# Key and query biases as one factor, query normalisation on GpSimd, and the statistics of x2 from two accumulators, in the attention loop of a macaron block

## The chip, the cores and the metric

The kernel runs on one core of a Trainium2 chip. The metric is the device time of one execution in microseconds (us), given as the median of several runs. Of the core's engines the text speaks by short names: PE is TensorE, DVE is VectorE, ACT is ScalarE, POOL is GpSimd, and SP is the engine whose queue issues most transfers.

## What is computed

The program is one block of three parts, each with a residual connection and a layer normalisation ahead of it: a mixture of experts, a causal linear attention, and the experts again with the same weights. All values are f32. There are 8 sequences of 1024 rows of 512 numbers, 64 tiles of 128 rows in all. Only the attention and the normalisation behind it are touched here. Cut to what matters:

```
x1 = x + 0.5 * ffn(layernorm(x))
q  = exp(layernorm(x1) @ Wq.T + bq)          # 16 heads of 32
k  = exp(layernorm(x1) @ Wk.T + bk)
v  = layernorm(x1) @ Wv.T + bv
num = q @ cumsum(outer(k, v))                # along the sequence
den = sum(q * cumsum(k))                     # for each head
x2  = x1 + (num / den) @ Wo.T + bo
out = x2 + 0.5 * ffn(layernorm(x2))
```

In num and den every product has one factor of q and one of k in the same dimension, so exp(bq) and exp(bk) can be multiplied in anywhere once. The kernel adds both biases into one tile, BK, at the start, and applies it to one of the two.

## The kernel before

The program has three stages in time: the first gate and experts, with the projections of x for q, k and v computed ahead and put in DRAM (to about 1010 us); the attention loop (to about 1915 us); the second experts, which stream their weights from DRAM again. Each engine runs its own instruction list, written out by hand, and semaphores order them. The change lies in the attention loop.

The loop index n runs over tiles of 128 rows. In one turn of the loop the engines work on several tiles at once: on the products of tile n, on the preparation of tile n + 1 (m in the code), on x2 of tile n - 1 and on the transposes of the normalised x2 of tile n - 2. The names used below are these.

- X1 is the tile after the first experts. PB[.][:, 0], [:, 1] and [:, 2] are q, k and v of a tile. DVE forms X1 and the three sums (L1132, and three adds through the helper L264), which read PSUM banks 4 to 7, and then the statistics of X1 (L1117, L1119, L1121).
- RS is one over the standard deviation, a power on POOL (L1203). ACT takes the exponentials of q and k (L1063, L1066) with it. KH is k rounded to the matmul's format (L1071, ACT), and KL the rest (L1206, POOL).
- UPTO and AFTER are triangular matrices. PE multiplies them with KH and KL into bank 2, which gives the running sum of k. DVE multiplies it with q into PR, reduces it to DEN (L1173), inverts that to RDEN (L1175), and multiplies q by it in place (L264, in the code the line with Q3).
- PE transposes k and q, ACT copies them to KT and QT (L1056, L1059), PE forms the scores S in banks 4 to 7, DVE masks them with TRI into ST (four instructions), and PE forms the attention output (semaphore s_av). ACT copies it to AT and rounds it to ATH (L1084, L1087), POOL forms the rest ATL (L1218), and PE multiplies by WO (12 matmuls `ps<-wo,s`, semaphore s_op).
- X2 is that product plus X1 with BO added (POOL, L1209), a sum on DVE. Its statistics are DVE's L1117, L1119 and L1121, one over its standard deviation POOL's L1214, the shift NM DVE's L1182, and the normalised XN3 ACT's L1093. PE transposes XN3 in the next turn.

PE may start the scores of tile n only when DVE has read banks 4 to 7 for tile n + 1, that is after X1 and the three sums. From n = 10 on every eighth turn also selects the best tokens of a finished sequence on DVE (the maximum, the replacement and the mask, then a turn later the weights), and the turns behind it gather them on PE.

Of the kernel before, what the change touches and what calls it, by code (L numbers as in the profile page):

```python
# [20 lines left out]
def macaron_block(nc, x, Wq, bq, Wk, bk, Wv, bv, Wo, bo, gate_w, gate_b, w1, w2, out):  # L21
    F = mybir.dt.float32
# [8 lines left out]
    EPS = 1e-5  # L31
# [9 lines left out]
    with ctx:  # L41
# [7 lines left out]
        def sem(name):  # L49
            return ctx.enter_context(nc.semaphore(name))  # L50
# [125 lines left out]
        def sems(name, n):  # L176
# [28 lines left out]
            "s_c", "s_x1", "s_tk", "s_tq", "s_tv", "s_x1st", "s_x1ag", "s_x1ve", "s_x1rs", "s_x1b"))  # L205
        s_kb, s_qe, s_ke, s_v, s_ktT, s_kt, s_qtT, s_qt, s_S, s_st, s_av, s_at = (sem(n) for n in (
            "s_kb", "s_qe", "s_ke", "s_v", "s_ktT", "s_kt", "s_qtT", "s_qt", "s_S", "s_st", "s_av", "s_at"))
# [4 lines left out]
        s_op, s_x2, s_x2st, s_x2ag, s_x2ve, s_x2rs, s_x2n, s_g3T, s_xt3, s_lg3, s_L3, s_fin, s_fout = (  # L212
            sem(n) for n in ("s_op", "s_x2", "s_x2st", "s_x2ag", "s_x2ve", "s_x2rs", "s_x2n", "s_g3T", "s_xt3", "s_lg3",
                             "s_L3", "s_fin", "s_fout"))
# [827 lines left out]
        def attention_act(act):  # L1042
# [3 lines left out]
            for v in range(6):  # L1046
                outer_act(act, v)
            for n in range(-2, NT + 9):
                live = 0 <= n < NT
# [3 lines left out]
                if live:  # L1053
                    act.wait_ge(s_ktT, n + 1)
                    act.wait_ge(s_S, 4 * n)
                    nc.scalar.copy(KT, ps[:, 0, :]).then_inc(s_kt, 1)  # L1056
                    act.wait_ge(s_qtT, n + 1)
                    act.wait_ge(s_av, n)
                    nc.scalar.copy(QT, ps[:, 1, :]).then_inc(s_qt, 1)  # L1059
                if nxt:  # L1060
                    act.wait_ge(s_tq, m + 1)
                    act.wait_ge(s_x1rs, m + 1)
                    nc.scalar.activation(PB[m % 4][:, 0, :], PB[m % 4][:, 0, :], ACT.Exp,  # L1063
                                         scale=RS[m % 2]).then_inc(s_qe, 1)
# [44 lines left out]
        def attention_dve(dve):  # L1109
            center_dve(dve)  # L1110
            dve.wait_ge(s_woh, 1)
            tt(WOL, WO, WOH.bitcast(F), ALU.subtract).then_inc(s_wol, 1)
            dve.wait_ge(s_bk, 1)

            def stats(i, src, s_src, s_st_, s_ag, s_ve, n):
                dve.wait_ge(s_src, n + 1)
                nc.vector.bn_stats(ST6[i], src).then_inc(s_st_, 1)  # L1117
                dve.wait_ge(s_st_, n + 1)
                nc.vector.bn_aggr(MV[i], ST6[i]).then_inc(s_ag, 1)  # L1119
                dve.wait_ge(s_ag, n + 1)  # L1120
                nc.vector.tensor_scalar(VE[i], MV[i][:, 1:2], EPS, None, ALU.add).then_inc(s_ve, 1)  # L1121

            for n in range(-2, NT + 9):
# [5 lines left out]
                if nxt:  # L1129
# [27 lines left out]
                if 0 <= n - 1 < NT:  # L1157
# [20 lines left out]
                if 0 <= n - 1 < NT:  # L1178
                    m = n - 1
                    dve.wait_ge(s_x2rs, m + 1)  # L1180
                    dve.wait_ge(s_x2n, m - 1)
# [11 lines left out]
        def attention_pool(pool):  # L1193
            pool.wait_ge(s_bo2, 1)
            for n in range(-2, NT + 2):
                m = n + 1
                if 0 <= m < NT:
                    pool.wait_ge(s_x1ve, m + 1)
                    pool.wait_ge(s_x2rs, n - 2)
                    pool.wait_ge(s_atl, n)  # L1200
                    for s_ in (s_kb, s_qe, s_v):
# [4 lines left out]
                    nc.gpsimd.tensor_tensor(KL, PB[m % 4][:, 1, :], KH.bitcast(F), ALU.subtract).then_inc(s_kl, 1)  # L1206
# [110 lines left out]
```

## Time and profile before

| what | value |
|---|---|
| median of 3 runs | 2622.75 us (2622.47 to 2626.64) |
| span of the profiled execution | 2617.3 us |
| busy: PE, DVE, ACT, POOL | 2133.4, 1008.2, 717.8, 368.0 us |
| instructions on POOL | 389 |
| chain that ended last: PE, DMA, DVE | 47%, 30%, 13% |
| between 1500 and 1600 us, in the loop: PE, DVE, ACT, POOL busy | 82.17, 86.12, 50.97, 36.85 us |

The profile gives the span from the first to the last instruction; it has no device time of its own, and the median of the runs is 5.4 us above the span. The busy shares over the whole span say little of the loop, where the stages behind and ahead of it hardly use DVE or POOL. The last line of the table is the loop alone.

### The profile page before, as it was taken

The numbers are of one execution on the slowest core, as the hardware profiler recorded it, in microseconds if no ns is written. First come the engines' busy times: TensorE is split into PE (matmuls) and PEld (weight loads), VectorE is DVE, ScalarE is ACT, GpSimd is POOL, SyncE is SP. The second block draws the span as 40 slices with busy tenths as digits, with TensorE's granted clock in tenths as the row PEclk, the third lists the DMA queues.
The fourth block names the chain that finished last, engine by engine and source line by source line (L and its number), as shares of the span: only waits on it lengthen the run. The fifth ranks groups of instructions, "written<-read, shape, count | busy, mean of one in ns | idle before, by whom it ended". The sixth has DMA issues, their size and how long they took to land.

```text
span 2617.3 us, 44159 instructions
## 1 busy us (share of the span) xinstructions
PE 2133.4 (82%) x18828; PEld 1247.7 (48%) x18828; DVE 1008.2 (39%) x1994; ACT 717.8 (27%) x1192; POOL 368.0 (14%) x389
## 2 busy tenths in 40 slices
PE   6979999999999998888788888887856656666665
PEld 3436665656666665666566666665611111111111
DVE  6831111111111113888888888888710000000006
ACT  5722111111111112454455445554410000000000
POOL 3210000000000000333343333333300000000000
PEclk9979999999999999998999989989978878888887
DMA  9759999999999994533333333333199999999998
GB/s 366 288 214 370 401 412 407 404 403 410 400 410 406 412 396 152 198 111 102 102 110 106 106 95 98 118 94 102 49 403 425 425 421 422 422 422 426 424 424 315
DMA packets 127458, 770.22 MB, mean 294 GB/s; under 512 B 11648, under 2 KB 11648, under 8 KB 74016
## 3 DMA queue, kind: packets, MB, share of 16 engines
q1 hardware_dynamic: 118048, 717.07, 69.7%
q10 hardware_dynamic: 9216, 50.34, 4.6%
q8 instruction: 149, 2.44, 0.4%
q14 instruction: 45, 0.37, 0.0%
HBM read 660.41 MB, written 100.66 MB: 291 GB/s over the span
## 4 chain that ended last, share of the span: by engine, by line
PE 47%; DMA 30%; DVE 13%; ACT 5%; issue 3%; POOL 1%; SPq 0%; DVEq 0%; ACTq 0%; POOLq 0%
PE ps L256 44%; DMA big<-in_L_ffn_w 29%; DVE big L264 6%; PE ps L260 2%; DVE big L1244 1%; DVE big L1117 1%; DVE big L1132 1%; DVE big L1173 1%; ACT big L1102 1%; ACT big L1084 1%; DMA xt_scratch<-big 1%; ACT big L1093 1%; POOL s L1206 1%; ACT big L1059 1%; DMA x_scratch<-big 1%
## 5 line engine op out<-in xcount | busy, mean ns | idle before, releaser
L256 PE MATMUL ps<-big 128*32 128x512 f32 (+5 forms) x13896 | 1103.4, 439 | 354.8 <-DMA big<-in_L_ffn_w 229.7
L256 PEld LDWEIGHTS ps<-big 128*32 128x32 f32 (+2 forms) x13896 | 416.0, 133 | 959.2 <-issue 547.9
L264 DVE TENSOR_TENSOR big<-ps,big 128x512 f32<-128x512 f32 (+1 forms) x629 | 382.7, 652 | 109.2 <-PE ps L256 104.8
L256 PE MATMUL ps<-wth,xth 128*128 128x512 f32 x768 | 309.0, 402 | 1.8 <-ACT big L792 1.7
L256 PE MATMUL ps<-wth,xtl 128*128 128x512 f32 x768 | 299.6, 390 | 0.0
L256 PE MATMUL ps<-wtl,xth 128*128 128x512 f32 x768 | 299.1, 389 | 0.0
L675 ACT ACTIVATE big<-ps 128x512 f32<-128x512 f32 x64 | 38.3, 598 | 833.4 <-PE ps L256 833.4
L699 DVE COPY big<-ps 128x128 f32<-128x128 f32 x64 | 18.3, 286 | 637.8 <-PE ps L635 637.8
L256 PE MATMUL ps<-wo,s 128*128 128x512 f32 x768 | 222.4, 445 | 1.4 <-ACT s L1087 1.4
L801 DVE TENSOR_SCALAR big<-ps,big 128x512 f32<-128x512 f32 x64 | 48.0, 750 | 407.4 <-PE ps L256 407.4
L256 PEld LDWEIGHTS ps<-wo,s 128*128 128x128 f32 x768 | 160.7, 217 | 45.4 <-issue 3.8
L1203 POOL TENSOR_TENSOR big<-big 128x1 f32<-128x1 f32 x64 | 35.2, 550 | 1003.3 <-DVE big L1121 1003.1
L260 PE MATMUL ps<-big 128*128 128x128 f32 x1032 | 146.9, 282 | 35.7 <-ACT big L472 16.5
L256 PEld LDWEIGHTS ps<-wth,xth 128*128 128x128 f32 x768 | 144.6, 188 | 54.6 <-issue 22.9
L264 DVE TENSOR_TENSOR xtl<-big,xth 128x512 fp32r<-128x512 f32 x64 | 44.1, 689 | 308.3 <-ACT xth L751 308.3
L256 PEld LDWEIGHTS ps<-wth,xtl 128*128 128x128 f32 x768 | 144.2, 188 | 31.2
L256 PEld LDWEIGHTS ps<-wtl,xth 128*128 128x128 f32 x768 | 144.4, 188 | 29.8 <-issue 1.9
L792 ACT ACTIVATE big<-ps,big 128x512 f32<-128x512 f32 x128 | 87.8, 689 | 244.1 <-PE ps L256 244.0
L260 PEld LDWEIGHTS ps<-big 128*128 128x128 f32 x1032 | 125.0, 145 | 58.6 <-issue 29.5
L1218 POOL TENSOR_TENSOR s<-big,s 128x512 fp32r<-128x512 f32 x64 | 84.0, 1313 | 181.6 <-ACT s L1087 181.5
L1206 POOL TENSOR_TENSOR s<-big,s 128x512 fp32r<-128x512 f32 x64 | 82.6, 1291 | 154.3 <-ACT s L1071 154.3
L256 PE MATMUL ps<-s,tri 128*128 128x512 f32 x240 | 88.4, 435 | 19.3 <-POOL s L1206 10.7
(91 smaller groups left out, 1584.0 us busy)
## 6 DMA issues: line engine op xcount, KB each, us to landing
big<-in_L_ffn_w SPq DMA_DIRECT2D x256, 2048.0 KB, 17.6
p_scratch<-big ACTq DMA_DIRECT2D x64, 768.0 KB, 10.3
big<-p_scratch SPq DMA_DIRECT2D x64, 768.0 KB, 4.3
big<-in_L_attn_x SPq DMA_DIRECT2D x16, 1024.0 KB, 12.7
xt_scratch<-big SPq DMA_DIRECT2D x16, 1024.0 KB, 10.4
big<-xt_scratch SPq DMA_DIRECT2D x16, 1024.0 KB, 16.0
big<-in_L_attn_x SPq DMA_DIRECT2D x64, 256.0 KB, 2.9
x_scratch<-big SPq DMA_DIRECT2D x64, 256.0 KB, 3.2
```

What stands on the lines that cost most here:

```text
L256: return nc.tensor.matmul(o, l, r, start=start, stop=stop, skip_group_check=True)
L260: t = nc.tensor.transpose(ps[:, k, 128 * j:128 * j + 128], src[:, 128 * j:128 * j + 128], IDN[:, :])
L264: return nc.vector.tensor_tensor(o, p, q, op)
L675: nc.scalar.activation(HG[e % 2], ps[:, 0, :], ACT.Gelu).then_inc(s_hg, 1)
L792: nc.scalar.activation(PST[t % 2][:, u, :], ps[:, 2 + q % 2, :], ACT.Identity, scale=STD[:, t:t + 1]).then_inc(s_pea, 1)
L801: nc.vector.tensor_scalar(PST[t % 2][:, 2, :], ps[:, 2 + q % 2, :], STD[:, t:t + 1], None, ALU.mult).then_inc(s_ped, 1)
L1059: nc.scalar.copy(QT, ps[:, 1, :]).then_inc(s_qt, 1)
L1084: nc.scalar.copy(AT, ps[:, 3, :]).then_inc(s_at, 1)
L1093: nc.scalar.activation(XN3[m % NX], X2, ACT.Identity, bias=NM[m % 2], scale=RS[2 + m % 2]).then_inc(s_x2n, 1)
L1203: nc.gpsimd.tensor_tensor(RS[m % 2], VE[m % 2], NHALF, ALU.pow).then_inc(s_x1rs, 1)
L1206: nc.gpsimd.tensor_tensor(KL, PB[m % 4][:, 1, :], KH.bitcast(F), ALU.subtract).then_inc(s_kl, 1)
L1218: nc.gpsimd.tensor_tensor(ATL, AT, ATH.bitcast(F), ALU.subtract).then_inc(s_atl, 1)
```

## The change

It does four things in the attention loop.

1. The bias tile BK is made into exp(bq + bk) once, on ACT. The key's exponential no longer takes a biased input: DVE's L1149 (multiply k by RS, add BK) is gone, and ACT applies RS as the scale of the exponential. In its place POOL multiplies q by BK (semaphore s_qb).
2. The multiplication of q by RDEN moves from DVE to POOL.
3. The statistics of X2 no longer come from DVE's three instructions. The sum that forms X2 also writes out the sum of its row (SX2). ACT takes the square of (SX2 - 512 x) with its sum over the row (SQ2), and writes the squares to where XN3 will be. POOL scales SQ2 and adds the epsilon, takes the power, and forms NM, which DVE did.
4. On ACT the key comes ahead of the query, the square stands ahead of the copy of XT3, and XN3 of tile n - 2 is written behind QT of turn n, where XN3 of tile n - 1 was written at the end of turn n.

```diff
+            act.wait_ge(s_bk, 1)
+            nc.scalar.activation(BK, BK, ACT.Exp).then_inc(s_eb, 1)
...
+                if 0 <= n - 2 < NT:
+                    t = n - 2
+                    act.wait_ge(s_nm, t + 1)
+                    nc.scalar.activation(XN3[t % NX], X2, ACT.Identity, bias=NM[t % 2],
+                                         scale=RS[2 + t % 2]).then_inc(s_x2n, 1)
                 if nxt:
-                    act.wait_ge(s_tq, m + 1)
+                    act.wait_ge(s_tk, m + 1)
                     act.wait_ge(s_x1rs, m + 1)
-                    nc.scalar.activation(PB[m % 4][:, 0, :], PB[m % 4][:, 0, :], ACT.Exp,
-                                         scale=RS[m % 2]).then_inc(s_qe, 1)
-                    act.wait_ge(s_kb, m + 1)
-                    nc.scalar.activation(PB[m % 4][:, 1, :], PB[m % 4][:, 1, :], ACT.Exp).then_inc(s_ke, 1)
+                    nc.scalar.activation(PB[m % 4][:, 1, :], PB[m % 4][:, 1, :], ACT.Exp,
+                                         scale=RS[m % 2]).then_inc(s_ke, 1)
...
+                    act.wait_ge(s_tq, m + 1)
+                    nc.scalar.activation(PB[m % 4][:, 0, :], PB[m % 4][:, 0, :], ACT.Exp,
+                                         scale=RS[m % 2]).then_inc(s_qe, 1)
...
+                if 0 <= n - 1 < NT:
+                    t = n - 1
+                    act.wait_ge(s_x2, t + 1)
+                    if t >= NX:
+                        act.wait_ge(s_mtok, 8 + (t - NX) // 8 + 1)
+                    nc.scalar.activation(XN3[t % NX], X2, ACT.Square, bias=SX2[t % 2], scale=-float(D),
+                                         accum_out=SQ2[t % 2]).then_inc(s_x2sq, 1)
...
-                if 0 <= n - 1 < NT:
-                    m = n - 1
-                    act.wait_ge(s_nm, m + 1)
-                    if m >= NX:
-                        act.wait_ge(s_mtok, 8 + (m - NX) // 8 + 1)
-                    nc.scalar.activation(XN3[m % NX], X2, ACT.Identity, bias=NM[m % 2],
-                                         scale=RS[2 + m % 2]).then_inc(s_x2n, 1)
@@ attention_dve
-                    nc.vector.scalar_tensor_tensor(out=PB[m % 4][:, 1, :], in0=PB[m % 4][:, 1, :], scalar=RS[m % 2],
-                                                   in1=BK, op0=ALU.mult, op1=ALU.add).then_inc(s_kb, 1)
...
-                    tt(X2, ps[:, 0, :], X1[m % 4], ALU.add).then_inc(s_x2, 1)
-                    stats(2 + m % 2, X2, s_x2, s_x2st, s_x2ag, s_x2ve, m)
+                    nc.vector.scalar_tensor_tensor(out=X2, in0=ps[:, 0, :], scalar=1.0, in1=X1[m % 4], op0=ALU.mult,
+                                                   op1=ALU.add, accum_out=SX2[m % 2]).then_inc(s_x2, 1)
...
-                    dve.wait_ge(s_qe, n + 2)
+                    dve.wait_ge(s_qb, n + 2)
...
+                    dve.wait_ge(s_qn, n + 1)
                     nc.vector.reciprocal(RDEN, DEN).then_inc(s_rcp, 1)
-                    dve.wait_ge(s_rcp, n + 2)
-                    tt(Q3, Q3, RDEN.unsqueeze(2).broadcast_to([128, 16, 32]), ALU.mult).then_inc(s_qn, 1)
...
-                    nc.vector.tensor_scalar(NM[m % 2], MV[2 + m % 2][:, 0:1], RS[2 + m % 2], -1.0, ALU.mult,
-                                            ALU.mult).then_inc(s_nm, 1)
@@ attention_pool
+                    pool.wait_ge(s_qe, m + 1)
+                    pool.wait_ge(s_kl, m + 1)
+                    nc.gpsimd.tensor_tensor(PB[j][:, 0, :], PB[j][:, 0, :], BK, ALU.mult).then_inc(s_qb, 1)
                     pool.wait_ge(s_x1st, m + 1)
-                    pool.wait_ge(s_kl, m + 1)
-                    nc.gpsimd.tensor_tensor(X1[m % 4], X1[m % 4], BO, ALU.add).then_inc(s_x1b, 1)
+                    pool.wait_ge(s_qb, m + 1)
+                    nc.gpsimd.tensor_tensor(X1[j], X1[j], BO, ALU.add).then_inc(s_x1b, 1)
+                    pool.wait_ge(s_rcp, m + 1)
+                    pool.wait_ge(s_x1b, m + 1)
+                    nc.gpsimd.tensor_tensor(Q3, Q3, RDEN.unsqueeze(2).broadcast_to([128, 16, 32]),
+                                            ALU.mult).then_inc(s_qn, 1)
...
+                    pool.wait_ge(s_x2sq, m + 1)
+                    pool.wait_ge(s_x2n, m - 1)
+                    pool.wait_ge(s_qn, min(n + 2, NT))
+                    nc.gpsimd.tensor_scalar(VE[2 + m % 2], SQ2[m % 2], 1.0 / D ** 3, EPS, ALU.mult,
+                                            ALU.add).then_inc(s_x2ve, 1)
                     pool.wait_ge(s_x2ve, m + 1)
-                    pool.wait_ge(s_x1b, min(n + 2, NT))
                     nc.gpsimd.tensor_tensor(RS[2 + m % 2], VE[2 + m % 2], NHALF, ALU.pow).then_inc(s_x2rs, 1)
+                    pool.wait_ge(s_x2rs, m + 1)
+                    nc.gpsimd.tensor_scalar(NM[m % 2], SX2[m % 2], RS[2 + m % 2], -1.0 / D, ALU.mult,
+                                            ALU.mult).then_inc(s_nm, 1)
                 if 0 <= n < NT:
                     pool.wait_ge(s_ath, n + 1)
-                    pool.wait_ge(s_x2rs, n)
+                    pool.wait_ge(s_nm, n)
                     nc.gpsimd.tensor_tensor(ATL, AT, ATH.bitcast(F), ALU.subtract).then_inc(s_atl, 1)
```

This is one turn on POOL before the change, in the middle of the loop. The rows are ATL of the turn before, RS of X1, KL, the addition of BO, and RS of X2:

```order
L1218 TENSOR_TENSOR s_68<-big,s_67 128x512 [waits s_x2rs,s_ath]
L1203 TENSOR_TENSOR big<-big 128x1 [waits s_qe,s_kb,s_v,s_atl,s_x1ve]
L1206 TENSOR_TENSOR s_66<-big,s_65 128x512 [waits s_x1rs,s_kh]
L1209 TENSOR_TENSOR big<-big 128x512 [waits s_kl,s_x1st]
L1214 TENSOR_TENSOR big<-big 128x1 [waits s_x1b,s_x2ve]
```

The same turn of the change on POOL. L1204 is q by BK, L1207 the addition of BO, L1210 q by RDEN, and L1217 to L1222 are the three small steps for X2:

```order
L1227 TENSOR_TENSOR s_68<-big,s_67 128x512 [waits s_nm,s_ath]
L1198 TENSOR_TENSOR big<-big 128x1 [waits s_ke,s_v,s_atl,s_x1ve]
L1201 TENSOR_TENSOR s_66<-big,s_65 128x512 [waits s_x1rs,s_kh]
L1204 TENSOR_TENSOR big<-big 128x512 [waits s_kl,s_qe]
L1207 TENSOR_TENSOR big<-big 128x512 [waits s_qb,s_x1st]
L1210 TENSOR_TENSOR big<-big 128x512 [waits s_x1b,s_rcp]
L1217 TENSOR_SCALAR big<-big 128x1 [waits s_qn,s_x2n,s_x2sq]
L1220 TENSOR_TENSOR big<-big 128x1 [waits s_x2ve]
L1222 TENSOR_SCALAR big<-big 128x1 [waits s_x2rs]
```

Five instructions in a turn became nine, and two of the four new ones are of 128x512. ATL now stands behind L1210 and the three small ones.

DVE before, from the masks of a turn to the first step of the next turn (L1149 is the biased key, the L264 with s_rcp is q by RDEN, L1182 is NM):

```order
L1149 SCALAR_TENSOR_TENSOR big<-big 128x512 [waits s_tk,s_x1rs]
L264 TENSOR_TENSOR big<-ps,big 128x512 [waits s_S] x4
L264 TENSOR_TENSOR big<-ps,big 128x512 [waits s_x2n,d_x20,s_x1b,s_op]
L1117 BN_STATS big<-big 128x6 [waits s_x2]
L1119 BN_AGGR big<-big 128x2 [waits s_x2st]
L1121 TENSOR_SCALAR big<-big 128x1 [waits s_x2ag]
L264 TENSOR_TENSOR big<-ps,big 128x512 [waits s_qe,s_upto]
L1173 TENSOR_REDUCE big<-big 128x16 [waits s_pr]
L1175 RECIPROCAL big<-big 128x16 [waits s_red]
L264 TENSOR_TENSOR big<-big 128x512 [waits s_rcp]
L1182 TENSOR_SCALAR big<-big 128x1 [waits s_x2rs]
L1132 SCALAR_TENSOR_TENSOR big<-ps,big 128x512 [waits d_x12,s_c]
```

The same stretch on DVE in the change (L1165 forms X2 with its sum, L1133 is X1 of the next turn):

```order
L266 TENSOR_TENSOR big<-ps,big 128x512 [waits s_S] x4
L1165 SCALAR_TENSOR_TENSOR big<-ps,big 128x512 [waits s_x2n,d_x21,s_x1b,s_op]
L266 TENSOR_TENSOR big<-ps,big 128x512 [waits s_qb,s_upto]
L1173 TENSOR_REDUCE big<-big 128x16 [waits s_pr]
L1176 RECIPROCAL big<-big 128x16 [waits s_qn,s_red]
L1133 SCALAR_TENSOR_TENSOR big<-ps,big 128x512 [waits d_x12,s_c]
```

Six instructions left DVE, and the product with q (the L266 that waits for s_upto) now waits for POOL's s_qb where it waited for ACT's s_qe.

## Rows read from the trace of the kernel before

**Rows 1.** The page, its span.

```profile
span 2617.3 us, 44159 instructions
```

**Rows 2.** Waits between 1180 and 1860 us: total us, times, longest.

```profile
PE ps L256 <- DVE big L264: 76.0, 27, 4.9
...
PE ps L256 <- ACT big L1059: 13.3, 24, 1.2
```

**Rows 3.** PE over eight tiles: start, length, work [idle before <-releaser].

```profile
1500.29 0.73 PE L256 MATMUL ps<-s,tri 128*128 128x512 f32 x2
...
1507.20 2.09 PE L256 MATMUL ps<-big 32*128 32x128 f32 x32 [4.92 <-DVE big L264]
1509.22 4.22 PE L256 MATMUL ps<-wo,s 128*128 128x512 f32 x12
...
1521.96 2.04 PE L256 MATMUL ps<-big 32*128 32x128 f32 x32 [2.60 <-DVE big L264]
1523.92 3.75 PE L256 MATMUL ps<-wo,s 128*128 128x512 f32 x12
...
1561.55 1.17 PE L256 MATMUL ps<-big 32*128 32x128 f32 x32 [2.39 <-DVE big L264]
...
1585.55 1.17 PE L256 MATMUL ps<-big 32*128 32x128 f32 x32 [1.45 <-DVE big L264]
1586.65 3.06 PE L256 MATMUL ps<-wo,s 128*128 128x512 f32 x12
...
1599.51 1.17 PE L256 MATMUL ps<-big 32*128 32x128 f32 x32 [0.33 <-ACT big L1059]
...
1607.54 0.73 PE L256 MATMUL ps<-s,tri 128*128 128x512 f32 x2
```

**Rows 4.** DVE over one turn without token selection.

```profile
1571.52 0.68 DVE L1132 SCALAR_TENSOR_TENSOR big<-ps,big 128x512 f32<-128x512 f32 x1
...
1575.66 0.75 DVE L1149 SCALAR_TENSOR_TENSOR big<-big 128x512 f32<-128x512 f32 x1 [0.45 <-POOL big L1203]
1576.33 3.07 DVE L264 TENSOR_TENSOR big<-ps,big 128x512 f32<-128x512 f32 x5
1579.44 0.69 DVE L1117 BATCH_NORM_STATS2 big<-big 128x6 f32<-128x512 f32 x1
...
1580.46 0.69 DVE L264 TENSOR_TENSOR big<-ps,big 128x512 f32<-128x512 f32 x1
...
1582.20 0.69 DVE L264 TENSOR_TENSOR big<-big 128x512 f32<-128x512 f32 x1
...
1582.93 0.68 DVE L1132 SCALAR_TENSOR_TENSOR big<-ps,big 128x512 f32<-128x512 f32 x1
```

**Rows 5.** DVE from the first step of the token selection to X1 behind it.

```profile
1500.74 1.22 DVE L322 MAX8 big<-big 32x8 f32<-32x1024 f32 x1
...
1504.57 0.69 DVE L1132 SCALAR_TENSOR_TENSOR big<-ps,big 128x512 f32<-128x512 f32 x1
```

**Rows 6.** ACT: an accumulator's read-out, AT, XN3, and an exponential behind RS.

```profile
1512.49 0.18 ACT L340 ACTIVATION_READ_ACCUMULATOR big<-big 32x1 f32 x1
...
1582.23 0.59 ACT L1084 COPY big<-ps 128x512 f32<-128x512 f32 x1 [1.52 <-PE ps L256]
...
1583.38 0.81 ACT L1093 ACTIVATE big<-big 128x512 f32<-128x512 f32 x1
...
1587.13 0.72 ACT L1063 ACTIVATE big<-big 128x512 f32<-128x512 f32 x1 [1.99 <-POOL big L1203]
```

**Rows 7.** POOL: one ATL at 1409 us, then a turn at 1586 us.

```profile
1409.46 1.60 POOL L1218 TENSOR_TENSOR s<-big,s 128x512 fp32r<-128x512 f32 x1 [2.88 <-ACT s L1087]
...
1586.49 0.55 POOL L1203 TENSOR_TENSOR big<-big 128x1 f32<-128x1 f32 x1 [1.66 <-DVE big L1121]
1589.22 1.28 POOL L1206 TENSOR_TENSOR s<-big,s 128x512 fp32r<-128x512 f32 x1 [2.19 <-ACT s L1071]
1590.65 1.28 POOL L1209 TENSOR_TENSOR big<-big 128x512 f32<-128x512 f32 x1
```

More of the change, by code:

```diff
@@ L170, in macaron_block @@
         BVT = SM[:, 224:228]
+        SX2 = [SM[:, 228 + i:229 + i] for i in range(2)]
+        SQ2 = [SM[:, 230 + i:231 + i] for i in range(2)]
         NG = NT // 4
@@ L205, in macaron_block @@
             "s_c", "s_x1", "s_tk", "s_tq", "s_tv", "s_x1st", "s_x1ag", "s_x1ve", "s_x1rs", "s_x1b"))
-        s_kb, s_qe, s_ke, s_v, s_ktT, s_kt, s_qtT, s_qt, s_S, s_st, s_av, s_at = (sem(n) for n in (
-            "s_kb", "s_qe", "s_ke", "s_v", "s_ktT", "s_kt", "s_qtT", "s_qt", "s_S", "s_st", "s_av", "s_at"))
+        s_eb, s_qb, s_qe, s_ke, s_v, s_ktT, s_kt, s_qtT, s_qt, s_S, s_st, s_av, s_at = (sem(n) for n in (
+            "s_eb", "s_qb", "s_qe", "s_ke", "s_v", "s_ktT", "s_kt", "s_qtT", "s_qt", "s_S", "s_st", "s_av", "s_at"))
         s_kh, s_kl, s_after, s_ath, s_atl, s_woh, s_wol = (sem(n) for n in (
@@ L211, in macaron_block @@
             "s_upto", "s_pr", "s_red", "s_rcp", "s_qn", "s_kv", "s_kva", "s_nm"))
-        s_op, s_x2, s_x2st, s_x2ag, s_x2ve, s_x2rs, s_x2n, s_g3T, s_xt3, s_lg3, s_L3, s_fin, s_fout = (
-            sem(n) for n in ("s_op", "s_x2", "s_x2st", "s_x2ag", "s_x2ve", "s_x2rs", "s_x2n", "s_g3T", "s_xt3", "s_lg3",
+        s_op, s_x2, s_x2sq, s_x2ve, s_x2rs, s_x2n, s_g3T, s_xt3, s_lg3, s_L3, s_fin, s_fout = (
+            sem(n) for n in ("s_op", "s_x2", "s_x2sq", "s_x2ve", "s_x2rs", "s_x2n", "s_g3T", "s_xt3", "s_lg3",
                              "s_L3", "s_fin", "s_fout"))
@@ L1112, in attention_dve @@
             tt(WOL, WO, WOH.bitcast(F), ALU.subtract).then_inc(s_wol, 1)
[L1113 to L1121, printed above, removed]
             for n in range(-2, NT + 9):
@@ L1136, in attention_dve @@
                         tt(PB[m % 4][:, u, :], ps[:, 4 + u, :], PB[m % 4][:, u, :], ALU.add).then_inc(s_, 1)
-                    stats(m % 2, X1[m % 4], s_x1, s_x1st, s_x1ag, s_x1ve, m)
+                    dve.wait_ge(s_x1, m + 1)
+                    nc.vector.bn_stats(ST6[m % 2], X1[m % 4]).then_inc(s_x1st, 1)
+                    dve.wait_ge(s_x1st, m + 1)
+                    nc.vector.bn_aggr(MV[m % 2], ST6[m % 2]).then_inc(s_x1ag, 1)
+                    dve.wait_ge(s_x1ag, m + 1)
+                    nc.vector.tensor_scalar(VE[m % 2], MV[m % 2][:, 1:2], EPS, None, ALU.add).then_inc(s_x1ve, 1)
                 if live and c < 7:
@@ L1145, in attention_dve @@
                         nc.vector.tensor_copy(KV[1], ps[:, 3, 0:128]).then_inc(s_kva, 1)
-                if nxt:
-                    dve.wait_ge(s_x1rs, m + 1)
-                    dve.wait_ge(s_tk, m + 1)
-                    nc.vector.scalar_tensor_tensor(out=PB[m % 4][:, 1, :], in0=PB[m % 4][:, 1, :], scalar=RS[m % 2],
-                                                   in1=BK, op0=ALU.mult, op1=ALU.add).then_inc(s_kb, 1)
                 if live:
@@ L1174, in attention_dve @@
                     dve.wait_ge(s_red, n + 2)
+                    dve.wait_ge(s_qn, n + 1)
                     nc.vector.reciprocal(RDEN, DEN).then_inc(s_rcp, 1)
-                    dve.wait_ge(s_rcp, n + 2)
-                    tt(Q3, Q3, RDEN.unsqueeze(2).broadcast_to([128, 16, 32]), ALU.mult).then_inc(s_qn, 1)
[L1178 to L1181, printed above, removed]
-                    nc.vector.tensor_scalar(NM[m % 2], MV[2 + m % 2][:, 0:1], RS[2 + m % 2], -1.0, ALU.mult,
-                                            ALU.mult).then_inc(s_nm, 1)
                 if n >= 10 and done == 0:
@@ L1194, in attention_pool @@
             pool.wait_ge(s_bo2, 1)
+            pool.wait_ge(s_eb, 1)
             for n in range(-2, NT + 2):
@@ L1197, in attention_pool @@
                 if 0 <= m < NT:
+                    j = m % 4
+                    Q3 = PB[j][:, 0, :].rearrange("p (h d) -> p h d", h=16)
                     pool.wait_ge(s_x1ve, m + 1)
-                    pool.wait_ge(s_x2rs, n - 2)
                     pool.wait_ge(s_atl, n)
-                    for s_ in (s_kb, s_qe, s_v):
+                    for s_ in (s_ke, s_qe, s_v):
                         pool.wait_ge(s_, m - 1)
@@ L1205, in attention_pool @@
                     pool.wait_ge(s_x1rs, m + 1)
-                    nc.gpsimd.tensor_tensor(KL, PB[m % 4][:, 1, :], KH.bitcast(F), ALU.subtract).then_inc(s_kl, 1)
+                    nc.gpsimd.tensor_tensor(KL, PB[j][:, 1, :], KH.bitcast(F), ALU.subtract).then_inc(s_kl, 1)
+                    pool.wait_ge(s_qe, m + 1)
+                    pool.wait_ge(s_kl, m + 1)
+                    nc.gpsimd.tensor_tensor(PB[j][:, 0, :], PB[j][:, 0, :], BK, ALU.mult).then_inc(s_qb, 1)
                     pool.wait_ge(s_x1st, m + 1)
-                    pool.wait_ge(s_kl, m + 1)
-                    nc.gpsimd.tensor_tensor(X1[m % 4], X1[m % 4], BO, ALU.add).then_inc(s_x1b, 1)
+                    pool.wait_ge(s_qb, m + 1)
[4 more added lines that the diff above has]
+                                            ALU.mult).then_inc(s_qn, 1)
                 m = n - 1
                 if 0 <= m < NT:
+                    pool.wait_ge(s_x2sq, m + 1)
[3 more added lines that the diff above has]
+                                            ALU.add).then_inc(s_x2ve, 1)
                     pool.wait_ge(s_x2ve, m + 1)
-                    pool.wait_ge(s_x1b, min(n + 2, NT))
                     nc.gpsimd.tensor_tensor(RS[2 + m % 2], VE[2 + m % 2], NHALF, ALU.pow).then_inc(s_x2rs, 1)
+                    pool.wait_ge(s_x2rs, m + 1)
+                    nc.gpsimd.tensor_scalar(NM[m % 2], SX2[m % 2], RS[2 + m % 2], -1.0 / D, ALU.mult,
+                                            ALU.mult).then_inc(s_nm, 1)
                 if 0 <= n < NT:
                     pool.wait_ge(s_ath, n + 1)
-                    pool.wait_ge(s_x2rs, n)
+                    pool.wait_ge(s_nm, n)
                     nc.gpsimd.tensor_tensor(ATL, AT, ATH.bitcast(F), ALU.subtract).then_inc(s_atl, 1)
```

1 line of the change is left out of this document (removed).

## The prediction

> **What bounds the kernel now.** I read the span first, then the waits inside the loop, then PE and DVE in order of time. The span is 2617.3 us [rows 1]; the median of the runs is 5.4 us above it. Costs below are differences in that one execution, and I take them off the median unscaled. The change touches only the attention loop, 64 turns. Behind the loop the second experts stream weights that can hardly start earlier than the loop's end, so what the loop gains should arrive at the end one to one.
>
> In the loop PE waits for DVE most: 76.0 us in 27 waits between 1180 and 1860 us, about 51 turns [rows 2]. Its waits for the copy QT are 13.3 us, mean 0.55.
>
> Eight turns, the period of the token selection, go from 1500.29 to 1607.54, that is 107.25 us or 13.4 a turn [rows 3]. In them PE stands 4.92, 2.60, 2.39 and 1.45 us for DVE, 11.36 together. Two of these waits are followed by slow matmuls: scores and output product take 2.09 + 4.22 and 2.04 + 3.75 us where a quick turn has 1.17 + 3.06. That is 2.08 and 1.56 us more.
>
> DVE itself needs 11.41 us a turn, from X1 at 1571.52 to X1 at 1582.93, with a single 0.45 us wait in it [rows 4]. Selection adds 3.83 us (1500.74 to 1504.57) [rows 5]. So DVE has no room: the selection turns push its work behind PE's, and it is two turns in catching up.
>
> **The change, part by part.**
>
> *DVE.* L1149 goes with its wait: from the wait's start, 0.45 before 1575.66, to 1576.33 are 1.12 us. The statistics of X2, 1579.44 to 1580.46, are 1.02. q by RDEN and NM, 1582.20 to 1582.93, are 0.73 [rows 4]. Together 2.87. The sum that forms X2 gets an accumulator. No DVE row shows one; between nothing and the 0.18 us of ACT's read-out [rows 6] I take 0.15. DVE needs 11.41 - 2.87 + 0.15 = 8.7 us a turn.
>
> *PE's own chain.* Take the end of the attention output as 0. PE's next scores need QT, and ACT makes AT, ATH, KT and QT for it one behind the other. AT and ATH are done 1.15 us after AT's start (XN3 follows at 1583.38, AT stood at 1582.23) [rows 6]; KT and QT are two more copies like AT's 0.59, and come a little closer behind each other, 1.2 together, and 0.1 leads to PE. XN3, 0.81 us, stood between ATH and KT and now stands behind QT. So the scores can start at about 2.5 us instead of 3.3. From the scores to the next turn's first matmul behind the output are 8.0 us (1599.51 to 1607.54) [rows 3]. A turn without extras is 10.5 to 10.6 us.
>
> *POOL's new loop.* Two 128x512 instructions and two small ones are added. A dependent large step takes 1.43 us from start to start (1589.22 to 1590.65) [rows 7]. The question is not POOL's busy time, 9 to 10 us, but a ring through it: RS 0.55 + 0.09 to ACT (1586.49 to 1587.13, [rows 6, 7]); exponential of k 0.75; KH 0.70 to POOL; KL 1.43; q by BK 1.33; on DVE product, reduction and reciprocal 1.74 (1580.46 to 1582.20, [rows 4]) and 0.05 back; q by RDEN 1.43; three small steps; ATL 1.43; RS again. Without the small ones that is 9.50 us. Their form with two constants is nowhere in this trace. From above each is bounded by the power's 0.55, from below by the 0.18 read-out, each with 0.14 for the semaphore. So three make 1.0 to 2.1, and the ring 10.5 to 11.6. I take 1.5, as they multiply and only one raises to a power: ring 11.0 us. It is 0.4 above PE's chain. The addition of BO (1.43) lies under DVE's 1.74.
>
> *q by RDEN on POOL.* Its operand RDEN is repeated 32 times from 16 numbers. On DVE that costs nothing: 0.69 like the others [rows 4]. I take the same on POOL. Bounds: the 1.28 of an ordinary one, and three times this, 3.84, argued below.
>
> *ACT.* The square (0.81 at most by the XN3 row) and its read-out (0.18) add 1.0 us where ACT otherwise waited for RS or the transposes; it needs X2, which is there at 7.3, and must be done when POOL has finished q by RDEN at about 10.5. It has 2 us of room. The listing of the change has no further table load inside the loop. The exponential of BK is once.
>
> *X1's turn.* BO's addition, now one step later, is needed a turn later.
>
> *Sum for eight turns.* DVE waits: the 2.60 and 1.45 go, but the scores then wait for QT, 0.35 in each of them. After a selection: without it, DVE would have X1 and its three sums read 1.1 us ahead of need (reciprocal at 9.4, 2.5 us of work, needed at 13.0); with 3.83 us PE waits 2.7 instead of 4.92. The 2.39 stays, since there DVE reduces what PE has just transposed. Saved: 2.60 + 1.45 + 2.2 - 0.7 = 5.55. The slow matmuls behind the 2.60 go: 1.56; those behind the selection stay. Of the waits for QT, 13.3 us over 51 turns is 2.1 in eight, all shorter on average than the 0.81 taken away: 2.1. Gross 9.2. Against it: the ring, 0.4 in four turns without extras, 1.6, and 0.1 to 0.3 of collisions. Net 7.4 us in eight turns, 59 in 64. The way out of the loop gets longer by about 1 us (square, two more POOL steps for 1.02 on DVE). **2622.75 - 58 = 2565 us.**
>
> **What a rule says.** One ATL took 1.60 us where KL, the same subtraction, takes 1.28 [rows 7]. The Trainium skill, page SBUF — State Buffer, section Who interferes with whom, says that a DVE instruction with two SBUF inputs and a GpSimd one that reads SBUF lock each other out for a whole instruction. By it, the change removes two such DVE instructions from each turn (biased key, q by RDEN) and leaves only those of the selection, so collisions would be rarer although POOL works nearly twice as long; the sum would keep the 0.1 to 0.3 above.
>
> The Trainium skill's page GPSIMD Engine Reference, section Engine selection, speaks against the change: two-input elementwise work belongs on VectorE, being about twice as slow on GpSimd. The trace agrees, 1.28 against 0.69 us. By that rule alone two moved steps would cost 1.2 us a turn; it is the ring below in which that would show.
>
> **The rivals.**
>
> *A, the forecast, 0.55.* The ring at about PE's chain. 2545 to 2590.
>
> *B, a dearer ring, 0.20.* If the four large steps in it take the 1.60 of the long ATL instead of 1.28, and the small ones 0.55, the ring is 11.6 + 1.3 = 12.9 us. Eight turns are 103 plus about 1.5 behind the selection, 104.5 against 107.25: 22 us gained, 2601. For it: POOL works through most of the turn, which no row shows. Against: the other two large rows here are 1.28.
>
> *C, slower, 0.10.* Only q by RDEN is dear, since POOL reads a repeated operand badly. The point where it decides: the ring must reach about 13.2 us, so this one instruction 1.28 + 2.2 = 3.5 us. At three times, 3.84, the ring is 13.6, eight turns 109 plus 1.5, 3.2 more than now, +26: 2649. For it: no POOL row has such an operand of 512 numbers. Against: DVE is indifferent to it.
>
> *D, a larger gain, 0.12.* The ring does not bind (small steps near 0.2) and PE's clock stays up also behind the selection: 9.2 + 2.08 in eight turns, 90 us: 2532. For it: DVE is idle for 2 us a turn and absorbs more. Against: 2.7 us of wait remain there.
>
> *E, no change, 0.03.* PE's waits for DVE turn one for one into waits for POOL's KL or q.
>
> **How the numbers follow.** B and D stand on both sides, so the range takes both in: 2525 to 2610. Outside are C and the tails. A difference of 0.2%, 5 us, is about what a measurement of this kernel can tell. Faster: A, B and D, 0.87. Slower: C, 0.10. Same: 0.03.
>
> **What the profile after would show.** Of 100 us in the loop (the table above), DVE's busy time down from 86 to about 72, POOL's up from 37 to between 75 and 85. PE's waits for DVE down from 76 to about 35 us in as many turns, those for QT to about 10. POOL's large steps 1.3 us each, the 128x1 ones under 0.55, the one with RDEN 1.3. A turn without extras 11 us. If the RDEN step is above 2 us, or PE waits for a product of POOL in most turns, the forecast is wrong by B or C. If DVE's sum with the accumulator takes far over 0.9, the DVE part is wrong.

## The result and the profile after

The changed kernel takes 2546.65 us (2542.3 to 2549.99, 4 runs) against 2622.61 us for the kernel before, measured beside it: ratio 0.971, 95% interval 0.9696 to 0.9724. That is 76 us less, where 58 were forecast. The profiled execution has a span of 2543.3 us, 74.0 less than before [rows 1].

The page of the changed kernel, its span and first section (busy us, share of the span, instructions):

```profile
span 2543.3 us, 44353 instructions
PE 2106.8 (83%) x18828; PEld 1228.6 (48%) x18828; DVE 855.2 (34%) x1674; ACT 765.5 (30%) x1321; POOL 554.0 (22%) x645
```

DVE lost 153 us of work and POOL took on 186. The last reduction of the loop starts at 1843.4 us; in the kernel before it started at 1916.2. So 72.8 of the 74.0 us are there by the end of the loop (2.8 of them stood before it began), and the second experts pass them on.

The waits of the changed kernel between 1180 and 1780 us, about 49 turns (total us, times, longest):

```profile
PE ps L258 <- DVE big L266: 41.5, 19, 3.3
...
PE ps L258 <- ACT big L1063: 11.3, 30, 0.5
...
PE ps L258 <- POOL s L1201: 3.8, 6, 0.8
```

In eight turns PE now waits 6.8 us for DVE, 1.8 for QT (L1063) and 0.6 for KL (L1201). By [rows 2] it was 11.9 and 2.1 for the first two, and the same view of the kernel before has this for KL, 1.1 us in eight turns:

```profile
PE ps L256 <- POOL s L1206: 7.0, 12, 0.7
```

PE in order of time over one group of eight turns (start, length, work, idle before it and its releaser), to set beside [rows 3]:

```profile
1412.69 0.75 PE L384 MATMUL ps<-big 128*128 128x128 f32 x4 [0.70 <-ACT big L1101]
...
1416.70 1.17 PE L258 MATMUL ps<-big 32*128 32x128 f32 x32 [2.39 <-DVE big L266]
1417.81 4.59 PE L258 MATMUL ps<-wo,s 128*128 128x512 f32 x12
...
1438.36 1.17 PE L258 MATMUL ps<-big 32*128 32x128 f32 x32 [0.33 <-ACT big L1063]
...
1443.30 0.50 PE L258 MATMUL ps<-s,tri 128*128 128x512 f32 x1 [0.57 <-POOL s L1201]
...
1465.05 1.24 PE L258 MATMUL ps<-big 32*128 32x128 f32 x32 [3.35 <-DVE big L266]
1466.22 4.50 PE L258 MATMUL ps<-wo,s 128*128 128x512 f32 x12
...
1477.94 1.17 PE L258 MATMUL ps<-big 32*128 32x128 f32 x32 [1.31 <-DVE big L266]
1479.04 3.04 PE L258 MATMUL ps<-wo,s 128*128 128x512 f32 x12
...
1511.90 0.75 PE L384 MATMUL ps<-big 128*128 128x128 f32 x4 [0.71 <-ACT big L1101]
```

L384 belongs to the gathered tokens and comes once in eight turns, so the group takes 99.2 us. The wait behind the selection fell from 4.92 to 3.35, the one behind it from 2.60 to 1.31, the 1.45 is gone, and the 2.39 stands as it was. The granted clock was 1.00 of full speed (the upper level, 2.4 GHz) from 1479 to 1482 us, behind the 1.31; it was 0.64 from 1466.2 to 1470.7 us, behind the 3.35, and 0.68 from 1417.0 to 1422.4 us, behind the 2.39, so part of each of these two stretches ran at the lower level, 1.2 GHz. In the kernel before it was 0.79 from 1524.0 to 1527.6 us, behind the 2.60.

POOL over one turn, and on to the next RS:

```profile
1439.86 0.55 POOL L1198 TENSOR_TENSOR big<-big 128x1 f32<-128x1 f32 x1
1441.95 1.29 POOL L1201 TENSOR_TENSOR s<-big,s 128x512 fp32r<-128x512 f32 x1 [1.55 <-ACT s L1078]
1443.38 1.27 POOL L1204 TENSOR_TENSOR big<-big 128x512 f32<-128x512 f32 x1
1444.80 1.27 POOL L1207 TENSOR_TENSOR big<-big 128x512 f32<-128x512 f32 x1
1446.54 1.05 POOL L1210 TENSOR_TENSOR big<-big 128x512 f32<-128x512 f32 x1 [0.47 <-DVE big L1176]
1447.78 0.19 POOL L1217 TENSOR_SCALAR big<-big 128x1 f32<-128x1 f32 x1 [0.19 <-POOL big L1210]
1448.06 0.55 POOL L1220 TENSOR_TENSOR big<-big 128x1 f32<-128x1 f32 x1
1448.70 0.26 POOL L1222 TENSOR_SCALAR big<-big 128x1 f32<-128x1 f32 x1
1449.12 1.26 POOL L1227 TENSOR_TENSOR s<-big,s 128x512 fp32r<-128x512 f32 x1
1450.51 0.55 POOL L1198 TENSOR_TENSOR big<-big 128x1 f32<-128x1 f32 x1
```

From RS to RS are 10.65 us, the length of the ring. L1210, q by RDEN, takes 1.05 us, less than an ordinary step, and the two small steps with constants take 0.19 and 0.26.

### The profile page after: what moved, and what is told of

Same layout as the page of the kernel before. It is cut to its first block, busy times and chain, and to the rows that moved or that the text cites. A ratio compares the mean times of both kernels' runs of the same rounds, so it can differ in the third digit from the quotient of the medians.

```text
span 2543.3 us, 44353 instructions
## 1 busy us (share of the span) xinstructions
PE 2106.8 (83%) x18828; PEld 1228.6 (48%) x18828; DVE 855.2 (34%) x1674; ACT 765.5 (30%) x1321; POOL 554.0 (22%) x645
## 4 chain that ended last, share of the span: by engine, by line
PE 47%; DMA 32%; DVE 7%; ACT 4%; POOL 4%; issue 3%; SPq 1%; POOLq 0%; DVEq 0%; ACTq 0%
PE ps L258 44%; DMA big<-in_L_ffn_w 30%; DVE big L266 2%; PE ps L262 2%; DVE big L1253 1%; SPq L18 1%; POOL s L1201 1%; DVE big L1173 1%; POOL s L1227 1%; DMA big<-in_L_attn_x 1%; POOL big L1210 1%; ACT big L1101 1%; DMA x_scratch<-big 1%; DVE big L1133 1%; DMA xt_scratch<-big 1%
## 5 line engine op out<-in xcount | busy, mean ns | idle before, releaser
L258 PE MATMUL ps<-big 128*32 128x512 f32 (+5 forms) x13896 | 1089.0, 434 | 313.7 <-DMA big<-in_L_ffn_w 227.9
L258 PEld LDWEIGHTS ps<-big 128*32 128x32 f32 (+2 forms) x13896 | 405.4, 129 | 916.6 <-issue 527.7
L266 DVE TENSOR_TENSOR big<-ps,big 128x512 f32<-128x512 f32 (+1 forms) x565 | 340.1, 649 | 141.4 <-PE ps L258 105.3
L258 PE MATMUL ps<-wo,s 128*128 128x512 f32 x768 | 213.5, 431 | 1.4 <-ACT s L1104 1.4
L258 PEld LDWEIGHTS ps<-wo,s 128*128 128x128 f32 x768 | 153.8, 207 | 42.0 <-ACT s L1104 1.6
L266 DVE TENSOR_TENSOR xtl<-big,xth 128x512 fp32r<-128x512 f32 x64 | 44.1, 689 | 314.6 <-ACT xth L753 314.6
L1201 POOL TENSOR_TENSOR s<-big,s 128x512 fp32r<-128x512 f32 x64 | 82.9, 1295 | 125.5 <-ACT s L1078 125.5
```

The costliest lines, as they stand in the source:

```text
L258: return nc.tensor.matmul(o, l, r, start=start, stop=stop, skip_group_check=True)
L266: return nc.vector.tensor_tensor(o, p, q, op)
L1201: nc.gpsimd.tensor_tensor(KL, PB[j][:, 1, :], KH.bitcast(F), ALU.subtract).then_inc(s_kl, 1)
```

## The experiments

Each kernel was timed in rounds with the kernel before on the same chip, in three sets on three chips; the changed kernel was not timed again beside them. The median of the kernel before was 2616 to 2621 us in these sets and 2623 us in the result above, so I compare ratios; a hundredth is 26 us. "Against the changed kernel" is the difference of the ratios from 0.971, in us.

| run | median us | ratio to before, interval | against the changed kernel |
|---|---|---|---|
| order alone | 2600.78 | 0.993, 0.9915 to 0.9945 | +58 |
| XN3 back | 2585.06 | 0.9871, 0.9856 to 0.9885 | +42 |
| KL doubled | 2619.2 | 0.9996, 0.9983 to 1.0008 | +75 |
| q by RDEN on DVE | 2563.11 | 0.9788, 0.977 to 0.9807 | +20 |
| statistics on DVE | 2578.05 | 0.9838, 0.9813 to 0.9862 | +34 |
| bias on DVE | 2553.84 | 0.9748, 0.9722 to 0.9773 | +10 |
| selection in three places | 2534.66 | 0.9664, 0.9641 to 0.9687 | -12 |
| later reduction | 2523.09 | 0.9633, 0.9606 to 0.966 | -20 |
| both moves | 2520.14 | 0.9637, 0.9614 to 0.9661 | -19 |
| short ring | 2546.72 | 0.9739, 0.9723 to 0.9755 | +8 |
| short ring, KL doubled | 2594.44 | 0.992, 0.9902 to 0.9938 | +55 |
| short ring, both moves | 2517.5 | 0.9622, 0.9605 to 0.964 | -23 |

### The order on ACT

The first run takes the kernel before and moves only XN3; the second takes the changed kernel and moves only XN3 back. That the key now comes ahead of the query and the square ahead of the copy of XT3 was not tested by itself.

```diff
                     nc.scalar.copy(QT, ps[:, 1, :]).then_inc(s_qt, 1)
+                if 0 <= n - 2 < NT:                       # e1; e2 does the reverse
+                    t = n - 2
+                    act.wait_ge(s_nm, t + 1)
...
+                    nc.scalar.activation(XN3[t % NX], X2, ACT.Identity, bias=NM[t % 2], scale=RS[2 + t % 2])
...
-                    nc.scalar.activation(XN3[m % NX], X2, ACT.Identity, bias=NM[m % 2], scale=RS[2 + m % 2])
```

> The kernel before, with one thing changed: XN3 of tile n - 2 is written behind QT of turn n on ACT. Theory 1 (the gain is DVE's relief): DVE still works 11.4 us a turn and PE's waits for it stay at about 76 us in the loop's middle; only the waits for QT (13.3 us in 51 turns) can go, so 2605 to 2620 us. Rival (the gain is this order alone): 2550 to 2570 us.

> The changed kernel, with XN3 of tile n - 1 again at the end of turn n, behind ATH. Theory 1: POOL has NM ready about 1.6 us after the end of the attention output, later than ATH (1.2), so KT and QT start about 1.2 us later than now in each turn in which QT is what PE waits for, some five of eight: +35 to +60 us, 2580 to 2605. If the order does not matter: 2547 within 5.

The order alone brings 0.7%, about 18 us, slightly more than theory 1 allowed and far less than the rival asked. Its waits for DVE between 1180 and 1780 us are 61.7 us in 46 turns, and DVE is as full as before (busy 87.8 us between 1500 and 1600 us, where it was 86.1). Without the order the changed kernel loses 42 us. Its longest group of waits is then the one for QT:

```profile
PE ps L258 <- ACT big L1063: 34.6, 34, 1.9
PE ps L258 <- DVE big L266: 31.2, 12, 2.9
```

And on ACT, in order of time, XN3 (L1103) is seen to stand for POOL's NM between ATH and KT:

```profile
1500.97 0.62 ACT L1099 CAST s<-big 128x512 fp32r<-128x512 f32 x1
1501.95 0.81 ACT L1103 ACTIVATE big<-big 128x512 f32<-128x512 f32 x1 [0.36 <-POOL big L1222]
1502.67 0.56 ACT L1060 COPY big<-ps 128x512 f32<-128x512 f32 x1
```

So the place of XN3 is worth 18 us by itself and 42 us once DVE is relieved. What hides behind DVE before the change shows after it. That is not the whole of the 42: put back, XN3 also waits for an NM that now comes from POOL (7.8 us in 18 of 46 turns, at most 11 us in 64), which in the kernel before came from DVE.

### Each part of DVE's relief undone

q by RDEN back on DVE behind the reciprocal; the statistics of X2 back on DVE (NM stays on POOL); the biased key back on DVE ahead of the masks, and no q by BK.

```diff
+                    tt(Q3, Q3, RDEN.unsqueeze(2).broadcast_to([128, 16, 32]), ALU.mult).then_inc(s_qn, 1)   # e4
...
+                    nc.vector.bn_stats(ST6[i], X2)                                                          # e5
+                    nc.vector.bn_aggr(MV[i], ST6[i])
+                    nc.vector.tensor_scalar(VE[i], MV[i][:, 1:2], EPS, None, ALU.add)
...
+                    nc.vector.scalar_tensor_tensor(out=PB[m % 4][:, 1, :], in0=PB[m % 4][:, 1, :],          # e6
+                                                   scalar=RS[m % 2], in1=BK, op0=ALU.mult, op1=ALU.add)
```

> The changed kernel, with q by RDEN back on DVE. Theory 1: DVE gets 0.6 to 0.7 us a turn more, which PE feels where it waits for DVE, in two of eight turns and the one behind them: +1.3 to 2 us in eight turns, 2557 to 2564. Rival (the ring binds): the ring loses about 0.9 us and the kernel gets faster, below 2540.

> The changed kernel, with the statistics of X2 back on DVE (the three instructions, no accumulator, no square on ACT); NM stays on POOL. Theory 1: DVE gets about 0.9 us a turn more, felt behind the selection and in the turn after it: +1.8 to 2.8 us in eight turns, 2561 to 2570. Rival (ACT's square and POOL's extra small step are a burden): faster than 2546.

> The changed kernel, with the key's bias back on DVE (L1149 of the kernel before, BK as a sum) and no q by BK on POOL. Theory 1: DVE gets 0.7 us and a wait for RS a turn more, +2 to 3.5 us in eight turns, 2562 to 2575. Rival (the ring binds): it loses 1.33 us of POOL and gains 0.75 of DVE, so no slower than 2546.

None gets faster, as all three should if the ring bound. But the costs do not follow DVE's time: 0.7 us a turn cost 20 us, 1.0 us cost 34 (more than I expected), and 0.75 us with a wait cost only 10 (less than I expected; the interval just meets that of the changed kernel). The difference fits the place. The first two stand between X2 and the three sums, which begin when PE's product is done and which PE's next scores wait for. The third stands ahead of the masks, where DVE waits for the scores anyway. PE's waits agree: between 1180 and 1780 us those for DVE are 56.6 us in 48 turns, 53.2 in 47 and 39.0 in 48, where the changed kernel has 41.5 in 49. What grew with the bias on DVE are the waits for KL, from 3.8 to 9.7 us, 8 us over 64 turns, for the key's exponential now waits for DVE. PE after the selection, with the bias on DVE and then with the statistics on DVE:

```profile
1471.41 2.02 PE L258 MATMUL ps<-big 32*128 32x128 f32 x32 [2.93 <-DVE big L266]
...
1484.34 1.17 PE L258 MATMUL ps<-big 32*128 32x128 f32 x32 [1.31 <-DVE big L266]
```

```profile
1478.48 2.09 PE L258 MATMUL ps<-big 32*128 32x128 f32 x32 [4.92 <-DVE big L266]
1480.50 4.06 PE L258 MATMUL ps<-wo,s 128*128 128x512 f32 x12
...
1492.92 2.09 PE L258 MATMUL ps<-big 32*128 32x128 f32 x32 [2.45 <-DVE big L266]
1494.94 3.69 PE L258 MATMUL ps<-wo,s 128*128 128x512 f32 x12
```

The first pair has waits close to those of the changed kernel (2.93 and 1.31 against 3.35 and 1.31), but its first scores are slow, 2.02 us against 1.24. The second has the waits (4.92 and 2.45 against 4.92 and 2.60 [rows 3]) and the slow matmuls of the kernel before. The statistics of X2 are the largest single part of DVE's relief.

### The ring through POOL

KL computed twice, one dependent step more; then the three small steps moved between RS and KL (and XN3 behind v on ACT); then both.

```diff
                     nc.gpsimd.tensor_tensor(RS[m % 2], VE[m % 2], NHALF, ALU.pow).then_inc(s_x1rs, 1)
+                t = n - 2                                  # e10, e11, e12: VE, RS and NM of X2 here
+                if 0 <= t < NT:
...
+                    nc.gpsimd.tensor_tensor(KL, PB[j][:, 1, :], KH.bitcast(F), ALU.subtract).then_inc(s_eb, 1)   # e3, e11
+                    pool.wait_ge(s_eb, m + 2)
                     nc.gpsimd.tensor_tensor(KL, PB[j][:, 1, :], KH.bitcast(F), ALU.subtract).then_inc(s_kl, 1)
```

> The changed kernel, with KL computed twice in a row on POOL, one dependent large step (1.43 us) more in the ring RS, exponential, KH, KL, q by BK, reduction, q by RDEN, NM, ATL. Theory 1 (the ring, 10.65 us, lies below PE's mean turn of 12.4): a ring of 12.1 costs only in the turns without extras, +5 to +35 us, 2552 to 2582. Rival (the ring binds as it stands): +1.43 in each of 64 turns, 2638.

> The changed kernel, with POOL's three small steps for X2 (1.3 us) taken out of the ring: they stand between RS and KL one turn later, where POOL waits 1.6 us for KH, and XN3 is written behind v on ACT. If the ring (now 9.3 us) touches PE only through the waits for KL (3.8 us in 49 turns) and after the selection: -5 to -12 us, 2534 to 2542. If the ring set the pace of the changed kernel as it stands: -1.3 us in most turns, below 2500. If it has nothing to do with it: 2547 within 4.

> The short ring with KL computed twice, a ring of 10.7 us like that of the changed kernel. If the doubled KL cost 73 us above because the ring became 12.1 us long: now it costs only what arrives late at PE, KL about 0.9 us later than in the changed kernel against 0.6 of slack, 2560 to 2590. If it is the lateness of KL at PE alone: again about 1.1 us a turn above the short ring, 2605 to 2620.

One more step cost 75 us, far above my range and near the rival's 91. PE's waits, 44 turns between 1180 and 1780 us:

```profile
PE ps L258 <- DVE big L266: 46.6, 18, 3.7
PE ps L258 <- POOL s L1203: 28.1, 31, 1.9
```

The waits for KL are 5.1 us in eight turns where they were 0.6. In three plain turns it is 12.01, 12.01 and 12.30 us from RS to RS (1412.25 to 1424.26, 1452.86 to 1477.17), about the 12.1 that I had counted for the longer ring: here the ring does set the pace. But the rival, that the ring set the pace already, is refuted by the short ring: with 1.3 us less in it, the waits for POOL vanish from the list of PE's waits and the kernel is no faster (0.9739, at or slightly above the changed kernel). With the short ring the doubled KL costs 47 us over the short ring (0.992 against 0.9739) instead of 75. Its waits for KL are 21.6 us in 46 turns, 3.8 in eight. The time, 2594.44 us, lies between my two ranges and decides for neither. The run was meant to have a ring of 10.7 us, so that only KL's lateness at PE was left to pay. Its rows show another ring that I had not counted:

```profile
1459.47 0.55 POOL L1198 TENSOR_TENSOR big<-big 128x1 f32<-128x1 f32 x1
...
1470.87 0.55 POOL L1198 TENSOR_TENSOR big<-big 128x1 f32<-128x1 f32 x1 [0.86 <-DVE big L1143]
```

From RS to RS are 11.40 us, and RS waits for DVE's last step of the statistics. This ring shares RS, the exponential, KH, KL and q by BK with the first, and then goes on DVE through the product, the reduction, the reciprocal, X1, the three sums and the statistics. In the changed kernel it takes 9.9 us, from RS at 1439.86 to the end of L1143 at 1449.80. That is below a plain turn; one large step more puts it above. So how the 75 us split between KL's lateness and the length of a ring is not shown: both rings and PE get KL late. The changed kernel, with 10.65 us, stands below the point from which POOL decides, and the kernel with 12.0 stands above it. My expectation compared the ring with the mean turn of 12.4 us. That was wrong: the extras behind the selection and the gathering lengthen the mean, but the ring stretches there too (16.95 us from RS to RS at the selection, 1490.38 to 1507.33, in the run with KL doubled), and the turn to compare with is the plain one of 10.5 us.

### What is left: DVE's extras ahead of the three sums

The selection in three places; the reduction of gathered tokens one turn later; both; both with the short ring.

```diff
                     nc.vector.tensor_scalar(VE[m % 2], MV[m % 2][:, 1:2], EPS, None, ALU.add).then_inc(s_x1ve, 1)
+                if n >= 10 and done == 0:                  # e7, e9, e12
+                    topk_max(dve, 8 + gb)
+                if n >= 10 and done == 1:
+                    topk_mask(dve, 8 + gb)
...
                 if n >= 10 and done == 0:
-                    topk_max(dve, 8 + gb)
                     topk_replace(dve, 8 + gb)
-                    topk_mask(dve, 8 + gb)
...
-                if n >= 10 and done == 4:                  # e8, e9, e12: done == 5, behind the three sums
+                if n >= 10 and done == 5:
                     merge_end_dve(dve, 8 + gb, 3)
```

> The changed kernel, with the selection on DVE in three places: the maximum behind the statistics of X1 in its turn, the replacement where it was, the mask behind the statistics of X1 one turn later. Theory 1 (what is left are DVE's extras in front of X1 and the sums): the 3.0 us wait behind the selection falls to about 0.3 and its slow matmuls (1.5 us) speed up, some 4 us in each of 7 groups of eight turns, 2510 to 2527 us. Rival (PE's own chain is all that is left): 2547 within 8.

> The changed kernel, with the reduction of the gathered tokens one turn later, behind the three sums of X1's tile, so that the sums no longer wait for PE's last transposes. Theory 1: the 2.39 us wait and its slow output product (4.6 against 3.0 us) go, about 3.5 us in each of 7 groups, 2518 to 2528 us. Rival: the wait comes back at the products that need bank 3, 2547 within 5.

> The changed kernel, with both moves of the two runs before: the selection in three places and the later reduction. If they do not touch each other, their gains add: 12 + 23.5 us below the changed kernel, 2508 to 2515. If the ring through POOL takes part back, less: up to 2525.

> The short ring with both moves. If the mask's and the weights' collisions with POOL were paid through the ring, the selection's move now brings its full 20 us or more: 2485 to 2505. If not: 2505 to 2512.

The later reduction did what it should: -20 us by the ratio, 23.5 by the medians. The selection in three places brought 12 us, where I expected 20 at the least. With it PE waits 0.94 us where it waited 3.35, but 2.10 a turn later, where it waited 1.31. POOL and DVE at that place show what happens (start and length, POOL first):

```profile
1459.06 1.58 POOL L1200 TENSOR_TENSOR big<-big 128x1 f32<-128x1 f32 x1 [1.08 <-DVE big L1143]
```

```profile
1459.02 1.22 DVE L266 TENSOR_TENSOR big<-big 32x1024 f32<-32x1024 f32 x1
...
1464.99 0.69 DVE L266 TENSOR_TENSOR big<-ps,big 128x512 f32<-128x512 f32 x1 [1.44 <-POOL big L1206]
...
1466.92 1.99 DVE L350 SCALAR_TENSOR_TENSOR big<-big 32x1024 f32<-32x1024 f32 x1
```

The mask starts just ahead of RS, and RS takes 1.58 us instead of 0.55. The ring is then late by 1.03, DVE stands 1.44 us for q by BK, and the weights are taken that much later. The weights themselves take 1.99 us, as they do in the changed kernel (1.28 in the kernel before). Both moves together are no better by the ratio than the later reduction alone, and did not reach the 2508 to 2515 us of gains that add. By the groups of eight turns they are better (95.5 us between two L384, against 96.1 with the later reduction and 99.2 in the changed kernel), but in the profiled execution the loop began 5.9 us later than in that of the later reduction (1026.8 against 1020.9 us). The lowest time is both with the short ring, 2517.5 us, 23 us below the changed kernel by the ratio. It lies outside both of my ranges, and its interval overlaps those of the later reduction and of both moves, so what the short ring adds to them cannot be told.

## Why the prediction was right, and where it was off

**DVE's relief: right.** DVE's 2.87 us went as counted; in the loop it is busy 74 us of 100 (72 forecast). Waits for DVE fell by 5.1 us in eight turns where 6.2 were forecast. The wait left behind the selection is 3.35 and not 2.7, the next 1.31 and not 0.35. In the turn of the second, DVE's weights run beside POOL's q by RDEN (start and length, DVE first):

```profile
1473.29 1.99 DVE L350 SCALAR_TENSOR_TENSOR big<-big 32x1024 f32<-32x1024 f32 x1
```

```profile
1473.15 1.05 POOL L1210 TENSOR_TENSOR big<-big 128x512 f32<-128x512 f32 x1 [0.93 <-DVE big L1176]
```

The weights take 2.01 us in the mean of six, against 1.28 in the kernel before. That would be 0.7 of the 1.0 us by which the wait exceeds the forecast; no run took this collision away. The 0.1 to 0.3 us that I set for collisions were too small; in the changed kernel ATL behind the mask takes 2.31 us once in eight turns, where it takes 1.26 in the rows above.

**PE's chain: right.** A turn without extras was forecast at 10.5 to 10.6 us; the plain turns from 1111.29 to 1132.25 us take 10.5 each. The place of XN3 was part of that step, and its worth was shown: 42 us in the changed kernel. But the waits for QT fell by 0.3 us in eight turns, where 2.1 less 0.7 were forecast: they stayed, 0.3 to 0.5 us each, in most turns.

**The slow matmuls: right in kind.** The output products behind the 2.60 us wait run fast again (3.04 against 3.75), those behind the selection and the gathering stay slow (4.50, 4.59), and of the selection's only the scores got faster (1.24 against 2.09; the product takes 4.50 against 4.22). The granted clock is 0.97 of full speed in each 100 us of the loop from 1200 to 1700 us, where it was 0.93 to 0.96 before.

**The ring: the mis-sized term.** "So three make 1.0 to 2.1, and the ring 10.5 to 11.6. I take 1.5 ... ring 11.0 us", and then "the ring, 0.4 in four turns without extras, 1.6". Measured, the small steps with their semaphores make 1.3, q by RDEN 1.24 instead of 1.43, and the ring 10.65. It is 0.1 above PE's chain and costs nothing: the short ring is no faster. Without the 1.6 the sum gives 9.0 in eight turns; the groups went from 108.2 us (mean of four, 1422.96 to 1855.62) to 99.0 (1387.84 to 1783.91). That is 9.2, my gross. Over the loop's eight groups the 1.6 is 13 of the 18 us by which I fell short, and 2.8 more stood before the loop began. That the gross comes out exactly is partly luck. Of its terms the waits for DVE gave 1.1 us too little and those for QT 1.1 too little; the slow matmuls gave 2.2 instead of 1.6 in the groups shown, and two waits that the sum left out fell as well, those for KL by 0.5 and those for ACT's biased copies for the gate (L1102, now L1112) by 0.7. POOL's busy time was over-counted too: 64 us of 100 in the loop (1300 to 1400 us), where 75 to 85 were forecast.

**The end of the loop.** I charged 1 us for the way out; from the last X2 to the last reduction it is 22.3 us now and before.

**The rivals.** B and C fell with POOL's rows: large steps 1.27 to 1.30 us but for single collisions, the repeated operand 1.05. D was half right: the ring did not bind, but the clock still falls behind the selection (0.64 of full speed), and of the 2.08 us that D added 0.57 came.

**Not settled.** How the 75 us of the doubled KL split between its lateness at PE and the two rings is open. That the selection's collision with RS is what took back its gain is read from the rows; no run had the mask free of the collision.

## What to carry to other kernels

Relief of an engine is worth what stands between its late release and what others wait for, not its busy time: 1.0 us of DVE's work in that stretch was worth 34 us, 0.75 us in DVE's own waiting time 10. When work moves to an idle engine, walk every ring of dependencies that it lies in and set each against a plain turn, not the mean one; a ring 0.1 us above the other chain was free, and one step more cost 75. An order that matters little under one bottleneck (18 us) can carry much of the gain once that is gone (42 us).

## What the hardware showed unexpectedly

POOL's multiplication with a repeated operand (16 numbers, each 32 times) took 1.05 us against 1.27 to 1.30 for whole operands of the same size. The sum on DVE with its accumulator cost 0.69 + 0.08 us. DVE instructions with two SBUF inputs and POOL's held each other up by about 0.7 to 1.05 us: a POOL power of 128x1 took 1.58 instead of 0.55 behind DVE's mask of 1.22 us. The Trainium skill, page SBUF — State Buffer, section Who interferes with whom, says that such a DVE instruction contends with a GpSimd instruction that reads SBUF, and that the port pair that the two share is an exclusive lock. The trace agrees, for a 128x1 instruction (1.58 us) as for a large one (ATL, 2.31 us).
